# Field-pair products as single 32-bit matmuls, with new order tables, in a recommendation tower on one core

## What is computed

```
e  = stack([tbl_f[ids[:, f]] for f in range(39)], axis=1)          # 512 x 39 x 16
x1 = einsum('bid,bjd,ijh->bhd', e, e,  W0.reshape(39, 39, 128))
x2 = einsum('bid,bjd,ijh->bhd', e, x1, W1.reshape(39, 128, 128))
z  = sum(concatenate([x1, x2], axis=1), axis=-1)                    # 512 x 256
h  = concatenate([z, dense_ctx], axis=1)                            # 512 x 272
h  = maximum(h @ W_top1 + b_top1, 0)
h  = maximum(h @ W_top2 + b_top2, 0)
y  = h @ W_top3                                                     # 512 x 1
```

## Time and profile before

| | us |
|---|---|
| three runs | 253.94, 254.91, 256.14; median 254.91 |
| profiled execution, span from first to last instruction | 356.0 |
| PE busy in it | 230.8 (65%) |
| DVE busy | 181.3 (51%) |
| ACT busy | 149.0 (42%) |
| POOL busy | 157.2 (44%) |
| mean granted TensorE clock | 0.832 |

### The profile page before, as it was taken

One profiled execution on the slowest core, in us unless ns is written; L12 is line 12 of the kernel. 1 busy time (PEld: TensorE's weight loads), 2 busy tenths in 40 slices (PEclk: granted clock), 3 DMA queues, 4 the chain that ended last, 5 costly groups with the idle time before them and its releaser, 6 DMA issues.

```text
span 356.0 us, 3918 instructions
## 1 busy us (share of the span) xinstructions
PE 230.8 (65%) x1198; PEld 179.7 (50%) x1212; DVE 181.3 (51%) x335; ACT 149.0 (42%) x284; POOL 157.2 (44%) x165
## 2 busy tenths in 40 slices
PE   0366000277475755855849595968758499999897
PEld 0212000155353533744638374757646378888696
DVE  1838000188465564625438457555646389876000
ACT  1134000156353443525335465335353467877502
POOL 5777777407374747370642717472737300000000
PEclk9999655579596968796967989898958589999989
DMA  7941100001010101010100102010101010011000
GB/s 198 295 110 13 19 6 6 4 3 25 7 21 10 18 12 17 14 16 3 24 4 10 17 4 24 6 24 3 24 5 24 5 16 11 13 18 19 3 0 2
DMA packets 27495, 9.40 MB, mean 26 GB/s; under 512 B 22497, under 2 KB 25569, under 8 KB 27474
## 3 DMA queue, kind: packets, MB, share of 16 engines
q1 hardware_dynamic: 22354, 7.86, 10.1%
q0 software_dynamic: 5120, 1.29, 4.3%
HBM read 6.50 MB, written 0.00 MB: 18 GB/s over the span
## 4 chain that ended last, share of the span: by engine, by line
PE 33%; issue 22%; another core or an unknown queue 21%; ACT 11%; DVE 7%; SPq 2%; DMA 1%; DVEq 0%; ACTq 0%
PE tower L655 7%; ACT prod_hi L482 5%; ACT dots L516 3%; PE copies L606 3%; DVE prod L404 3%; PE sums L620 3%; PE sums L621 3%; PE sums L622 3%; DVE prod_lo L412 2%; PE ring L646 2%; PE ring L644 2%; DMA bt_sb<-bt 1%; PE tower L671 1%; PE ring L634 1%
## 5 line engine op out<-in xcount | busy, mean ns | idle before, releaser
L332 POOL DMA_INDIRECT gathered<-table,rows x160 | 156.9, 981 | 122.3 <-DVE parts L383 74.7
L404 DVE TENSOR_TENSOR prod<-first,copies 128x512 f32<-128x512 f32 x96 | 64.2, 682 | 99.4 <-issue 90.7
L412 DVE TENSOR_TENSOR prod_lo<-prod,prod_hi 128x512 fp32r<-128x512 f32 x96 | 64.6, 686 | 25.3 <-issue 16.6
L516 ACT COPY dots<-ring 128x320 f32<-128x320 f32 x64 | 43.3, 736 | 63.4 <-remote 55.7
L606 PE MATMUL copies<-turned,sel_sb 128*128 128x512 bf16 x98 | 39.4, 442 | 46.8 <-issue 40.7
L482 ACT CAST prod_hi<-prod 128x512 fp32r<-128x512 f32 x96 | 57.0, 624 | 10.7 <-DVE prod L404 5.6
L655 PEld LDWEIGHTS tower<-dots,w_sb 128*128 128x128 f32 x312 | 51.6, 213 | 11.9 <-issue 7.2
L655 PE MATMUL tower<-dots,w_sb 128*128 128x128 f32 x312 | 53.5, 299 | 6.4 <-ACT dots L516 6.3
L620 PE MATMUL sums<-prod_hi,w_hi 128*128 128x512 f32 x96 | 51.0, 531 | 1.2 <-issue 0.8
L621 PE MATMUL sums<-prod_lo,w_hi 128*128 128x512 f32 x96 | 42.2, 440 | 0.0
L622 PE MATMUL sums<-prod_hi,w_lo 128*128 128x512 f32 x96 | 41.8, 435 | 0.0
(11 more groups left out here) (85 smaller groups left out, 233.5 us busy)
## 6 DMA issues: line engine op xcount, KB each, us to landing
gathered<-table,rows POOLq DMA_INDIRECT x160
diag<-columns SPq DMA_DIRECT2D x128, 20.0 KB
wt_sb<-wt SPq DMA_DIRECT2D x2, 512.0 KB
sel_f<-sel SPq DMA_DIRECT2D x1, 448.0 KB
w0a<-w_ij SPq DMA_DIRECT2D x1, 448.0 KB
w0b<-w_ji SPq DMA_DIRECT2D x1, 448.0 KB
ids_sb<-ids SPq DMA_DIRECT2D x1, 85.0 KB, 2.0
ident_f<-ident SPq DMA_DIRECT2D x1, 64.0 KB
```

Source lines behind the costliest of these rows:

```text
L332: pool.indirect_dma_start(gathered[0:n, k % NGATHER, q, :], None, table, bass.IndirectOffsetOnAxis(ap=rows[0:n, k, q:q + 1], axis=0)).then ...
L404: nc.vector.tensor_tensor(prod[:, m % NPROD, :], first[:, k % 2, :], copies[n % 3][:], ALU.mult)\
L412: nc.vector.tensor_tensor(prod_lo[:, m % NPART, :], prod[:, m % NPROD, :], prod_hi[:, m % NPART, :], ALU.subtract).then_inc(lo_ready, 1)
L516: nc.scalar.copy(dots[:, g % 2, :, at:at + SUB].rearrange("p i b -> p b i"), ring[n % 2][:, 0:SUB * WIDE].rearrange("p (b i) -> p b i", i= ...
```

## The change

The float32 product goes to PE as it is: one float32 matmul for each tile with the float32 weights `w0a`, in place of three float32r ones. The casts `high`, the subtractions `low`, `prod_hi`, `prod_lo`, their `NPART` ring and the semaphores between them go. `NPROD` is 8 instead of 5, and a product buffer comes free when PE has used it. The squares are 12 rows, squared by ACT and used by one float32 matmul over 12 rows; their cast and subtraction go. The three instructions that make parts of W0 go. The tables `TENSOR`, `SCALAR` and `VECTOR` have new numbers; the group tables, `diag`, the dots, the second layer, the tower, SP and POOL are as before. The core of the diff (declarations left out):

```diff
-    for n in range(3):
-        for i in range(LEFT):
-            ij[TILES, FIELDS * n + i] = i * FIELDS + i
+    for i in range(LEFT):
+        ij[TILES, i] = i * FIELDS + i
...
-TENSOR = dict(first=-3.51, second=(-3.43, -3.32, -3.09, -2.19, -1.71, -0.56),
-              tile=(-0.0, 1.0, 2.0, 3.0, 4.0, 6.0), sum_squares=5.68, columns=-0.86, x1=8.68,
+TENSOR = dict(first=-6.0, second=(-5.0, -3.9, -2.7, -1.5, -0.4, 0.8),
+              tile=(-2.3, -1.1, 0.1, 1.2, 2.4, 3.6), sum_squares=3.0, columns=-0.86, x1=5.6,
...
-        NPROD, NPART, NGATHER, NTURN = 5, 7, 3, 3
+        NPROD, NGATHER, NTURN = 8, 3, 3
...
-            dve.wait_ge(ready, 4)
-            nc.vector.tensor_copy(w0_hi[:], w0a[:]).then_inc(ready, 1)
-            dve.wait_ge(ready, 5)
-            nc.vector.tensor_tensor(w0_lo[:], w0a[:, 0:TILES, :], w0_hi[:, 0:TILES, :], ALU.subtract).then_inc(ready, 1)
-
-            nc.vector.tensor_tensor(w0_hi[QUAD:2 * QUAD, TILES, :], w0a[QUAD:2 * QUAD, TILES, :],
-                                    w0_hi[QUAD:2 * QUAD, TILES, :], ALU.subtract).then_inc(ready, 1)
...
                 if m >= NPROD:
 
-                    dve.wait_ge(lo_ready, m - NPROD + 1)
+                    dve.wait_ge(tile_used, m - NPROD + 1)
...
-            def low(k, t):
-                m = TILES * k + t
-                dve.wait_ge(hi_ready, m + 1)
-                if m >= NPART:
-                    dve.wait_ge(tile_used, m - NPART + 1)
-                nc.vector.tensor_tensor(prod_lo[:, m % NPART, :], prod[:, m % NPROD, :],
-                                        prod_hi[:, m % NPART, :], ALU.subtract).then_inc(lo_ready, 1)
...
-                nc.scalar.copy(prod_hi[:, m % NPART, :], prod[:, m % NPROD, :]).then_inc(hi_ready, 1)
...
-                nc.scalar.activation(square[:, k % 2, :], first[:, k % 2, :], ACT.Square).then_inc(squared, 1)
-                act.wait_ge(squared, k + 1)
-                nc.scalar.copy(square_parts[:, k % 2, :], square[:, k % 2, :]).then_inc(square_hi, 1)
+                nc.scalar.activation(square[0:LEFT, k % 2, :], first[0:LEFT, k % 2, :], ACT.Square).then_inc(squared, 1)
...
-                pe.wait_ge(lo_ready, m + 1)
-                hi, lo = prod_hi[:, m % NPART, :], prod_lo[:, m % NPART, :]
-                to = sums[k % 2][:]
-                pe.matmul(to, w0_hi[:, t, :], hi, start=(t == 0), stop=False)
-                pe.matmul(to, w0_hi[:, t, :], lo, start=False, stop=False)
-                pe.matmul(to, w0_lo[:, t, :], hi, start=False, stop=(t == TILES - 1)).then_inc(tile_used, 1)
+                pe.wait_ge(prod_ready, m + 1)
+                pe.matmul(sums[k % 2][:], w0a[:, t, :], prod[:, m % NPROD, :],
+                          start=(t == 0), stop=(t == TILES - 1)).then_inc(tile_used, 1)
...
-                pe.wait_ge(square_ready, k + 1)
-                pe.matmul(sums[k % 2][:], w0_hi[:, TILES, :], square_parts[:, k % 2, :], start=False, stop=False)\
+                pe.wait_ge(squared, k + 1)
+                pe.matmul(sums[k % 2][:], w0a[0:LEFT, TILES, :], square[0:LEFT, k % 2, :], start=False, stop=False)\
```

More of the change, by code:

```diff
@@ L113 @@
 STEPS = TILES + 1
-TENSOR = dict(first=-3.51, second=(-3.43, -3.32, -3.09, -2.19, -1.71, -0.56),
-              tile=(-0.0, 1.0, 2.0, 3.0, 4.0, 6.0), sum_squares=5.68, columns=-0.86, x1=8.68,
[L116 to L120, removed]
+TENSOR = dict(first=-6.0, second=(-5.0, -3.9, -2.7, -1.5, -0.4, 0.8),
+              tile=(-2.3, -1.1, 0.1, 1.2, 2.4, 3.6), sum_squares=3.0, columns=-0.86, x1=5.6,
+              dot=(8.5, 8.8, 10.1, 10.6))
+SCALAR = dict(first=-5.2, squares=1.0, sums=4.6, columns=0.41, x1=6.6, dot=(9.5, 10.4, 11.3, 12.2))
+VECTOR = dict(product=(-4.1, -3.0, -1.8, -0.6, 0.5, 1.7), split=(-9.6, -9.2, -8.4, -8.1, -7.9), columns=0.9, x1=6.9)
 GROUP_TENSOR = (dict(layer2=6.22, rate=2.58, tower=(23.18, 26.7, 31.41)),
@@ L183, in build @@
         w0b = sb("w0b", [P, TILES + 1, P])
-        w0_hi = sb("w0_hi", [P, TILES + 1, P], F32R)
-        w0_lo = sb("w0_lo", [P, TILES, P], F32R)
         first = sb("first", [P, 2, COLS])
         prod = sb("prod", [P, NPROD, COLS])
-        prod_hi = sb("prod_hi", [P, NPART, COLS], F32R)
-        prod_lo = sb("prod_lo", [P, NPART, COLS], F32R)
         square = sb("square", [P, 2, COLS])
-        square_parts = sb("square_parts", [P, 2, COLS], F32R)
         x1 = sb("x1", [P, COLS])
@@ L252, in build @@
         prod_ready = sem("prod_ready")
-        hi_ready = sem("hi_ready")
-        lo_ready = sem("lo_ready")
         tile_used = sem("tile_used")
         squared = sem("squared")
-        square_hi = sem("square_hi")
-        square_ready = sem("square_ready")
         square_used = sem("square_used")
@@ L446, in _ @@
             for what in dve_order:
-                {"split": split, "columns": columns_low, "product": product, "low": low,
-                 "squares": square_low, "x1": turned_low, "h1": h1_sum}[what[0]](*what[1:])
+                {"split": split, "columns": columns_low, "product": product, "x1": turned_low, "h1": h1_sum}[what[0]](*what[1:])
             dve.wait_ge(tower_in, 16 * 7)
@@ L473, in store_first, with square_first @@
                 nc.scalar.copy(first[:, k % 2, :], copies[n % 3][:]).then_inc(first_ready, 1)
[L475 to L481, removed]
-                nc.scalar.copy(prod_hi[:, m % NPART, :], prod[:, m % NPROD, :]).then_inc(hi_ready, 1)
-            def square_both(k):
+            def square_first(k):
                 act.wait_ge(first_ready, k + 1)
                 if k >= 2:
-                    act.wait_ge(square_ready, k - 1)
                     act.wait_ge(square_used, k - 1)
-                nc.scalar.activation(square[:, k % 2, :], first[:, k % 2, :], ACT.Square).then_inc(squared, 1)
-                act.wait_ge(squared, k + 1)
-                nc.scalar.copy(square_parts[:, k % 2, :], square[:, k % 2, :]).then_inc(square_hi, 1)
+                nc.scalar.activation(square[0:LEFT, k % 2, :], first[0:LEFT, k % 2, :], ACT.Square).then_inc(squared, 1)
             def store_x1(k):
@@ L545, in _ @@
                 {"columns": store_columns, "first": store_first,
-                 "high": high, "squares": square_both, "sums": store_x1, "x1": store_turned,
+                 "squares": square_first, "sums": store_x1, "x1": store_turned,
                  "dot": store_dots, "tower": tower_step}[what[0]](*what[1:])
@@ L611, in add_tile @@
                 if t == 0:
-                    pe.wait_ge(ready, 7)
+                    pe.wait_ge(ready, 4)
                     if k == 0:
```

## The result

The change makes the kernel slower: 270.79 us (267.88 to 272.20) against 254.47 (253.94 to 256.14) for the kernel before on the same chip, a ratio of 1.061 [1.055, 1.067], that is 16.3 us more. The profiled execution took 271.59 us with a span of 269.8: 1.8 us lie around the span. Here the time agrees with the span but for that, so the rows can be read directly, which those of before could not.

A forecast was written before the change was run, and what follows sets the result against it. POOL's gathers, 12.5 us a block, and the tail bound the kernel before; PE would bind after. From block 6, 92.9 + 2 + 146.0 + 19.4 + 3.7 gave 264.0, taken as 263 us, range 250 to 276.

The forecast's parts named there:

- the mechanism itself: PE becomes the bound from the second group on and the kernel slower: 263 us, own range 258 to 270, chance 0.52.
- the 3.7 us: Gap between the 251.2 us summed for the kernel before and its median, given to landing or what lies around the span.
- slower gathers would not fit into 254.91: In the sum for the kernel before: gathers slower than 1.25 us each would exceed the median of 254.91 us.
- The binding wait is the one at block 6: DVE's wait for gathered data at block 6's split decides the end, with PE full behind it: 264 us against block 15's 259.
- The 264.0: End time counted from block 6's split: 92.9 + 2 + 146.0 of PE work + 19.4 + 3.7 us.
- 12 rows or 117 make no difference to the columns: Square matmul on PE: priced by columns whatever its row count, so +0.645 us each.
- A little off: Changes between matmuls of different kinds on PE partly go, so 263 us was taken below the counted 264.
- The clock: Rival: PE's pauses in the first blocks halve its clock, 20 us a block; two such blocks give 278 us; chance 0.14.
- POOL waiting for splits by the end: Sign that the forecast is right: late in the run, GpSimd's gathers wait for DVE's splits; no size given.
- POOL issuing without a break up to the end: Sign that the forecast is wrong: GpSimd issues gathers without pause until the end; no size given.
- No change: Rival: gathers stay the bound and PE catches up, so the end is the last split's tail, 255 to 257 us; chance 0.18.
- faster: Rival: pauses in the exchange between PE, ACT and DVE set the time before; 244 to 251 us after; chance 0.16.

The follow-up runs named there:

- the nine-gather kernel: The kernel before with nine gathers a block instead of ten, the last field column of each quad left at zero: 237.11 us, ratio 0.927.

## Why the prediction was right, and where it was off

The direction and the mechanism held. 270.79 lies in the range of 250 to 276, but 0.8 above the 258 to 270 given for the mechanism itself, and 7.8 above the 263.

- *The gathers bound the kernel before: shown.* One gather less in ten takes 19.7 us off, beside the forecast's 1.25 x 16. *Its sum was right for a partly wrong reason.* Of the 3.7 us that I gave to landing or what lies around the span, 1.8 lie around the span; the rest is that gathers were not at 1.25, less a tail that was shorter than I had it. With the 981 ns of the kernel before and the 0.30 between two, gathers come every 1.284, so the last starts at 3.36 + 159 x 1.284 = 207.5 and not at 202.1. With the 2.9 to the last split, the tail of 44.1 that the nine-gather kernel shows (I had 45.8) and the 1.8 that gives 256.3, an estimate, beside 256.83 on that chip. The kernel before with ten gathers has no trace without pauses. The sentence "slower gathers would not fit into 254.91" was wrong.
- *The Trainium skill, "SBUF — State Buffer", section "Who interferes with whom",* says that a DVE instruction with two SBUF inputs contends with a GpSimd instruction that reads SBUF. I gave that at most 5 us and leaned to none. The trace agrees with the rule: 987 ns with the subtractions, 951 to 952 in three kernels without them, 5.1 us in all, in gathers that begin while a subtraction runs and not in those that begin under a cast. And as the forecast said, the end stayed that of PE, so the 5 us gave nothing.
- *A tile takes 0.875 us: right*, 0.86 measured, inside the bounds of 0.85 and 0.88.
- *DVE and ACT's relief costs and gives nothing: right.* 125 us less of busy time, and the kernel is slower.
- *The binding wait is the one at block 6: right.* DVE waits 5.05 us at that split, 0.61 at the next and not at all at the later ones; PE waits 2.14 us at block 6, then not again before the tail, and is busy for 139.32 of 140 us.
- *The 264.0 was 7.6 too low: several terms of one sum.* In the span it was 92.9 + 2 + 146.0 + 19.4 = 260.3, and the trace has 94.81 + 2 + 155.2 + 17.8 = 269.8. The split of block 6 begins 1.9 later: its last gather ends at 91.82 and not at 90.9, and the split begins 2.99 us behind that and not 2. At blocks 1 to 5 and 7 that distance is 1.35 to 1.49; why it was twice as long at the one block that counts stays open. (Where expectations above take 4 us for it, they took the gather before the last for the last.) The last layers are 1.6 shorter. PE's list took 155.2 (96.8 to 252.01) where I counted 146.0. Of these 9.2, the squares are 11 x 0.39 = 4.3 ("12 rows or 117 make no difference to the columns" was right for the columns and wrong for the price), the waits of the tail 0.68 + 1.58 + 0.77 = 3.0, for which this sum had nothing, and the stretch at 246.39 with the clock at 0.50 another 1.3; 0.6 is left over. The 3.7 were 1.8. Together 264.0 + 9.5 - 1.9 = 271.6, the time of the profiled execution.
- *"A little off" for changes between kinds of matmul* had the wrong sign. A block took 14.32 us from one x1 to the next (rows below) with 18 layer-2 matmuls of 0.22 in it, so 10.36 against the 10.06 of the count, and the 0.39 of the square is more than that difference.

```profile
108.06 0.60 PE L584 MATMUL ring<-ident_f,x 128*128 128x128 f32 x4
...
122.38 0.60 PE L584 MATMUL ring<-ident_f,x 128*128 128x128 f32 x4
```

- *The clock: right to be a rival, and it did fall, but where it cost little.* At block 2 PE waits 3.71 us, and from 44 to 46 us the granted clock is 0.59 (0.56 in the next 2 us, then 1.00): the tile at 44.50 takes 1.87 us up to the next start and not 0.86. PE still had time to wait at blocks 3 to 6 (0.34, 1.28, 1.55 and 2.14 us), so that was made up; at those waits, and at the 2.54 of block 1, the clock did not fall. From 100 to 240 it is 1.00. It falls once more in the tail, behind waits of 0.68 and 1.58 us, to 0.50 from 246 to 248, for the 1.3 us above. Two blocks at half clock, the price of this rival, did not come. "TensorE: Matmul & The Clock Gate", section "HAM oscillation — how this bites in real kernels", in the Trainium skill describes a kernel that loses the clock in each wait between its bursts; the trace agrees at the longest wait, 3.71 us, and in the tail, and shows none lost at the waits of 0.34 to 2.54 us.

```profile
44.50 2.08 PE L571 MATMUL sums<-prod,w0a 128*128 128x512 f32 x2 [3.71 <-DVE prod L383]
...
46.37 1.06 PE L559 MATMUL copies<-turned,sel_sb 128*128 128x512 bf16 x2
```

- *"POOL waiting for splits by the end" did not come, and "POOL issuing without a break up to the end" was listed as a sign that I was wrong.* It was a poor sign. The last gather starts at 203.27 and its split at 213.42 in the timeline: some 9 us of slack that three buffers of ten gathers hold without stopping POOL. The sign to read is the split's own wait: gone from block 8 on.
- *No change, or faster:* ruled out by the result. The reason given for faster, pauses in the exchange that hold the time before, is ruled out by the kernel before with nine gathers, at 237.11 where it asked for 250.

## What to carry to other kernels

Here, taking work from engines that didn't set the end bought nothing, and since it was paid on the engine that was next in line, the kernel got slower as soon as that engine passed the bound: PE went from 8.3 to over 10 us of a block, and with layer 2 beyond the gathers' 12.5. Before a list is priced by its columns, look at whether each matmul has the rows of its neighbours, and add the tail's waits to the sum. To see which of two resources binds, take a tenth of one away: the full saving, half of it or nothing says up to where it binds. And to find what delays an instruction, compare the ones that begin under a suspect with the ones that don't: that needs no further run.

## What the runs showed of the hardware that was not expected

- *A matmul of two float32 operands* is two records of 0.43 us for 512 columns at full clock, 0.86 against 0.69 for three float32r ones, and with 12 rows among matmuls of 128 it costs 0.39 us more.
- *A gather that begins while DVE subtracts one SBUF buffer from another* takes longer by what is left of the subtraction less about 0.12 us: up to 1.46 us and not 0.94.
- *One program has two conditions.* The same kernel took 253 to 259 us in some sets of runs and 340 to 364 in others, one of the two throughout a set, and one chip showed both. In the second GpSimd stops between its gathers while DVE waits for what the profile names as nothing or remote. It is not the clock alone (0.841 over the run), and the pauses end where the gathers do. An example from the kernel before, beside the earlier trace rows: ACT's first copy waits 32.26 us, though the group of copies by PE to which the one it reads belongs starts at 33.57 and is over at 34.39.

```profile
33.57 0.82 PE L606 MATMUL copies<-turned,sel_sb 128*128 128x512 bf16 x3 [1.78 <-issue]
...
63.77 0.59 ACT L473 COPY first<-copies 128x512 f32<-128x512 f32 x1 [32.26 <-remote]
```

What makes a set of runs fall into it was not tried and stays open. The trace that the prediction was read from was such an execution, and the timed runs were not: prices of single instructions and gather intervals carried over, waits did not.
